# Cross-attention and routed experts on one core: another order of one attention turn on all five engines

## The chip, the cores and the metric

The kernel runs on one core of a Trainium2 chip, as one program on its five engines: TensorE (matmuls and transposes), VectorE, ScalarE, GpSimd and SyncE, which here only issues DMAs. The engines run side by side, each in the order in which its own instructions are written, and wait for each other on semaphores. The metric is the device time of one execution in microseconds, as the median of several.

## What is computed

For x and a context of 64 x 64 rows of 256 numbers:

```python
x = x + attention(layernorm(x), ctx)       # 16 heads of 16, keys and queries RMS-normed
x = x + experts(layernorm(x))              # 8 experts, 2 of them for each row
# attention: q = rms(ln(x) @ Wq + b) * nq;  k = rms(ctx @ Wk + b) * nk;  v = ctx @ Wv + b
#            softmax(q k^T / 4) v, for each head and sequence, then @ Wo + b
# (the text half of the context is empty: 64 rows are fewer than 257)
# experts:   logits = ln(x) @ gate; softmax, best two, weights normed to 1
#            each: (silu(x W1g) * (x W1u)) @ W2, summed with the weights
```

## The kernel before

The 4096 rows are 32 tiles of 128. **Stage one** handles the attention of a tile, picks its experts and sends each row, normed, with its weight, to two places of a buffer in HBM that is sorted by expert. **Stage two** loads that buffer in 72 slots of 128 rows and runs the experts. The change touches stage one alone.

Stage one is a pipeline of 38 **turns**, written out with no planner: `turns_sp` calls each engine's `turn(j, s)`, with turn number i = 4j + s. In one turn an engine works on several tiles, each in another phase. `tile(lag)` is tile i - lag (a negative lag is a tile ahead), on GpSimd and SyncE it is `Tile(j, s - lag)`. The order of the calls in `turn` is the engine's order of work, and nothing else sets it. Buffers are doubled by the tile's parity, so nearly each step also waits until the tile two before it has been read. All matmuls with full precision are done with operands split into a high and a low part: ScalarE makes the high part (`..._hi`), VectorE or GpSimd the low one (`..._lo`).

What a tile passes through, with the names and lines of the profile:

- `ln1_stats`, `ln1_mean` (VectorE, L819, L824) give mean and variance. GpSimd's `ln1` gives the reciprocal root (`inv_sqrt`: an add L413, then a power L415) and the shift (L422). ScalarE's `ln1_norm` (L548) norms.
- `tr_x` (L1134) transposes on TensorE, `xt_hi` (L542) and `xt_lo` (L829) split.
- The context: SyncE's `load_ctx` (L322), ScalarE's `ctx_hi` (L569), GpSimd's `ctx_lo` (L401).
- `project_kv` and `project_q` (L1117 to L1125): queries, keys, values. `k_square`, `q_square` (L593, L599) sum squares on ScalarE. GpSimd's `qk_rms` turns them into **r_qk**, the reciprocal roots for query and key (add L413, 128x2; power L415, 128x2). `k_scale` (ScalarE, L628) and `q_scale` (VectorE, L883) apply it.
- `tr_k` (L1143), `k_hi` (L554), `k_lo` (L835): keys transposed and split. `tr_q` (L1150), `q_hi` (L564, four copies), `q_lo` (L841): the queries. Both use one PSUM bank, so `tr_q` waits until `k_lo` has read the keys.
- `score_max` (L1165): rough scores. `find_max` (L846), `neg_max_hi`, `neg_max_lo` (L852, L857), `tr_max` (L1206), `neg_max_rows` (L586): negated maxima. `score` (L1227 to L1231): the scores with these added. `softmax_exp` (L621).
- SyncE's `spread_v` (L335) lays the values out block by block; `weigh` (L1177) multiplies, `invert_sums`, `normalise` (L864, L870), `tr_att` (L1212), `att_hi`, `att_lo` (L615, L877), `project_out`; `residual` (L892 to L899) adds and takes the second norm's statistics.
- GpSimd's `ln2` (L413, L415), VectorE's `ln2_norm` (L905) and ScalarE's `row_copy` (L581) make the rows. `choose` (L914 to L927, even turns), `count_rows`, `route` (L934 to L949, odd turns) find the places of two tiles. `gap_exp` (L635) and GpSimd's `weights` (L442 to L446) give the expert weights.
- GpSimd's `send` writes the row numbers (L451) and issues two indirect DMAs (L457), one for each of a row's two experts, six turns after the tile's projections.

The expert weights are also loaded and split in stage one, one 32nd a turn (`load_weights`, `weights_hi` L574, `weights_lo` L407).

Of the kernel before, what the change touches and what calls it, by code (L numbers as in the profile page):

```python
# [24 lines left out]
NT = T // P  # L25
# [20 lines left out]
SKEW = 4  # L46
# [39 lines left out]
def build_in(nc, stack, x, ctx_t, w_proj, w_out, w_exp, w_gate, bias, norm_q, norm_k, out,  # L86
# [216 lines left out]
    def _(sp):  # L303
# [39 lines left out]
        def turn(j, s):  # L343
            if Tile(j, s + 2).live:
                load_ctx(Tile(j, s + 2))
# [9 lines left out]

        turns_sp(sp, turn)
# [30 lines left out]
    def _(pool):  # L387
# [22 lines left out]
        def inv_sqrt(t, out_, tmp, in_, scale, eps, ready, mid, done_):  # L410

            need_alone(pool, pool_passed, ready, t.n + 1)
            pool.tensor_scalar(tmp, in_, scale, eps, ALU.mult, ALU.add).then_inc(mid, 1)  # L413
            need_alone(pool, pool_passed, mid, t.n + 1)
            pool.tensor_tensor(out_, tmp, half_neg[:, 0:tmp.shape[1]], ALU.pow).then_inc(done_, 1)  # L415

        def ln1(t):
            need_alone(pool, pool_passed, S["xn_ready"], t.n - 1)
            inv_sqrt(t, rstd[:, t.slot, :], veps[:, t.slot, :], mean_var[:, t.par, 1:2], 1.0, 1e-5,
                     S["ln1_mean"], S["ln1_veps"], S["ln1_rstd"])  # L420
            need_alone(pool, pool_passed, S["ln1_rstd"], t.n + 1)
            pool.tensor_scalar(shift[:, t.par, :], mean_var[:, t.par, 0:1], rstd[:, t.slot, :], -1.0, ALU.mult, ALU.mult  # L422
                               ).then_inc(S["ln1_shift"], 1)

        def qk_rms(t):
# [3 lines left out]
            inv_sqrt(t, r_qk[:, t.par, :], ms_eps[:, t.par, :], sumsq[:, t.par, :], 1.0 / D, 1e-6,  # L429
                     S["k_squared"], S["qk_veps"], S["qk_rstd"])  # L430

        def ln2(t):
            need_alone(pool, pool_passed, S["row_ready"], t.n - 1)
            inv_sqrt(t, rstd2[:, t.slot, :], veps2[:, t.par, :], mean_var2[:, t.par, 1:2], 1.0, 1e-5,
                     S["ln2_mean"], S["ln2_veps"], S["ln2_rstd"])
# [12 lines left out]
        def send(t):  # L448
# [3 lines left out]
                             ).then_inc(S["ids_set"], 1)  # L452
            need_alone(pool, pool_passed, S["ids_set"], t.n + 1)
            need_alone(pool, pool_passed, R["place_set"], t.pair + 1)
            need_alone(pool, pool_passed, R["weight_set3"], t.pair + 1)
            for k in range(2):
                pool.indirect_dma_start(  # L457
                    sorted_rows, bass.IndirectOffsetOnAxis(ap=place_i[:, t.slot // 2, k, t.par:t.par + 1], axis=0),
                    row[:, k, t.slot, :], None, bounds_check=ROWS - 1, oob_is_err=False
                ).then_inc(row_sent[t.slot], 16)  # L460
# [35 lines left out]
        ln1(Tile(0, 0))  # L496
        ln1(Tile(0, 1))
# [21 lines left out]
        for q in (qp_h, qp_l):  # L519
            pool.memset(q[:, :, :, :, :, :].rearrange("p u b c g l -> p (u b c g l)").bitcast(F32), 0.0  # L520
                        ).then_inc(q_cleared, 1)
        turns_sp(pool, turn)
# [15 lines left out]
    def _(act):  # L538
# [99 lines left out]
        def turn(j, s):  # L638
# [7 lines left out]
            if tile(0).live:  # L646
                xt_hi(tile(0))
            if tile(1).live:
                k_hi(tile(1))
            if tile(-1).live:  # L650
                ln1_norm(tile(-1))
            if tile(-1).live:
                ctx_hi(tile(-1))
            if tile(1).live:
                t = tile(1)
                t.first = isinstance(j, int) and t.n == 0
                q_hi(t)
            if tile(2).live:
                neg_max_rows(tile(2))
            if tile(0).live:  # L660
# [3 lines left out]
            if tile(3).live:  # L664
                att_hi(tile(3))
            if tile(0).live:
                v_copy(tile(0))
            if tile(0).live:
                weights_hi(tile(0))
                k_scale(tile(0))  # L670
            if tile(4).live:
                row_copy(tile(4))
            if tile(2).live:
                softmax_exp(tile(2))
            if s % 2 == 1 and tile(5).live:
                gap_exp(tile(5), tile(4), (s - 5) // 2 % 2)
# [16 lines left out]
        ln1_norm(t)  # L693
        split_hi(1)
# [50 lines left out]
    def _(dve):  # L745
# [144 lines left out]
        def residual(t):  # L890
# [5 lines left out]
            dve.bn_stats(stats2[:, t.par, :], x1[:, t.at, :]).then_inc(S["ln2_stats"], 1)  # L896
            need(dve, S["row_ready"], t.n - 1)
# [53 lines left out]
        def turn(j, s):  # L951
# [8 lines left out]
            ahead = tile(-2) if tile(-2).live else None  # L960
            if tile(0).live:
                xt_lo(tile(0))
            if isinstance(j, int) and j == s == 0:
                rest_of_setup()
            if tile(1).live:
                k_lo(tile(1))
            if tile(2).live:
                find_max(tile(2))
            if ahead:
                n = j * SKEW + s + 2 if isinstance(j, int) else None  # L970
                ln1_stats(ahead, {2: x_second, 8: x_third, 9: x_rest}.get(n))
            if tile(2).live:
                neg_max_hi(tile(2))
            if tile(3).live:
                invert_sums(tile(3))
            if tile(2).live:
                neg_max_lo(tile(2))
            if tile(3).live:
                normalise(tile(3))
            if ahead:  # L980
                ln1_mean(ahead)
            if tile(1).live:
                q_lo(tile(1))
            if tile(4).live:
                ln2_norm(tile(4))
# [4 lines left out]
            if isinstance(j, int) and j == s == 0:  # L990
                fold_gate()
            if tile(0).live:
# [453 lines left out]
```

## Time and profile before

| | |
|---|---|
| three runs, median (lowest to highest) | 549.66 us (548.14 to 552.85) |
| the profiled execution | 549.9 us, span 548.1 |
| busy share of the span: TensorE, VectorE, ScalarE, GpSimd | 80%, 75%, 58%, 55% |
| between 250 and 300 us: TensorE, VectorE, ScalarE, GpSimd busy | 45.8, 44.5, 36.7, 36.2 of 50 us, granted clock 1.00 |
| chain that ended last | TensorE 62%, VectorE 12%, issue 7%, ScalarE 5%, GpSimd 5% |
| longest waits, 60 to 310 us | ScalarE q_hi for TensorE tr_q 34.2 us in 27; ScalarE neg_max_rows for tr_max 22.6; GpSimd send for its own row numbers 19.7; GpSimd's r_qk add for the squares 19.5; ScalarE k_scale for r_qk 10.4 |
| one find_max (L846) | 1.22 us |
| one indirect DMA of L457 on GpSimd | 0.97 to 1.25 us, 64 in all |

"Busy" is time in which an instruction of the engine runs. A wait is put down to the engine whose semaphore came last. The first attention turns start near 12 us, the last query transposes are at 313 us, GpSimd's last send ends at 347.8, and stage two ends at 548.

### The profile page before, as it was taken

Reading aid. Unit: us, or ns where it says so; the run is one execution under the profiler, and the core shown is the slowest. Engines: PE = TensorE matmul, PEld = TensorE weight load, DVE = VectorE, ACT = ScalarE, POOL = GpSimd, SP = SyncE. Lnnn points to the kernel's source line nnn. Section 1 sums busy time; section 2 is a strip of 40 time slices with the busy share of each in tenths; the row PEclk is TensorE's granted clock in tenths of the full one; section 3 lists DMA queues with packets and bytes.
Section 4 is the critical chain, followed back from the end, with each engine's and each line's share of the span. In section 5 each row is a group of like instructions: output and inputs, shape, how many; then the busy total and the mean of one; then the engine's idle time right before and its main releaser. Section 6 shows DMA issues by size and latency. Waiting matters only on the chain.

```text
span 548.1 us, 14646 instructions
## 1 busy us (share of the span) xinstructions
PE 438.2 (80%) x4120; PEld 389.1 (71%) x4120; DVE 413.4 (75%) x1359; ACT 315.5 (58%) x934; POOL 303.5 (55%) x531
## 2 busy tenths in 40 slices
PE   2879889898989998898989772299999999999100
PEld 1668778777877877787778661199999999899100
DVE  7458888988988898889888867066767676676384
ACT  5357777767776867686777531155656666565000
POOL 6634467777777677767776646224444444444200
PEclk9989999999999999999999986599999999999655
DMA  7231432222322222222222113524444444331499
GB/s 232 53 111 40 133 129 83 73 65 80 88 67 72 74 82 73 77 78 77 79 72 74 50 50 94 149 81 129 124 123 126 119 121 126 111 115 66 168 401 351
DMA packets 49560, 60.51 MB, mean 110 GB/s; under 512 B 7616, under 2 KB 43083, under 8 KB 49483
## 3 DMA queue, kind: packets, MB, share of 16 engines
q1 hardware_dynamic: 38026, 38.00, 23.7%
q0 software_dynamic: 6528, 16.86, 8.8%
q10 hardware_dynamic: 4928, 4.72, 2.6%
q8 instruction: 37, 0.61, 0.5%
q14 instruction: 41, 0.33, 0.2%
HBM read 32.86 MB, written 23.27 MB: 102 GB/s over the span
## 4 chain that ended last, share of the span: by engine, by line
PE 62%; DVE 12%; issue 7%; ACT 5%; POOL 5%; DMA 4%; SPq 2%; another core or an unknown queue 0%; POOLq 0%; ACTq 0%; DVEq 0%
PE bank L1117 11%; PE bank L1118 11%; PE bank L1119 11%; PE bank L1328 4%; DMA we_l<-expert_out 3%; PE bank L1177 3%; PE bank L1125 3%; PE bank L1150 3%; PE bank L1227 2%; DVE late L835 2%; PE bank L1231 2%; PE bank L1228 2%; PE bank L1229 2%; PE bank L1165 2%; PE bank L1357 1%
## 5 line engine op out<-in xcount | busy, mean ns | idle before, releaser
L527 POOL DMA_INDIRECT expert_out<-probs,late x72 | 70.0, 972 | 94.4 <-ACT probs L720 60.1
L457 POOL DMA_INDIRECT sorted_rows<-row,place_i x64 | 66.0, 1031 | 36.2 <-POOL row L451 24.5
L564 ACT CAST qp_h<-bank 32x256 f16<-32x256 f32 x128 | 46.4, 363 | 40.8 <-PE bank L1150 38.5
L841 DVE TENSOR_TENSOR qp_l<-bank,qp_h 32x256 f16<-32x256 f32 x128 | 53.7, 419 | 9.8 <-ACT qp_h L564 6.6
L1117 PE MATMUL bank<-we_h,xt_h 128*128 x144 | 53.4, 371 | 0.1
L1075 DVE SCALAR_TENSOR_TENSOR probs<-xn,late,bank 128x128 f32<-128x128 f32 x72 | 25.0, 347 | 36.2 <-issue 16.9
L708 ACT ACTIVATE xn<-bank 128x176 f32<-128x176 f32 x72 | 22.9, 318 | 42.7 <-PE bank L1119 35.2
L1118 PE MATMUL bank<-we_l,xt_h 128*128 x144 | 47.1, 327 | 0.0
L1119 PE MATMUL bank<-we_h,xt_l 128*128 x144 | 46.9, 326 | 0.0
L1067 DVE TENSOR_TENSOR xt_l<-bank,xt_h 128x256 fp32r<-128x256 f32 x72 | 30.5, 424 | 21.3 <-ACT xt_h L702 17.5
L1328 PE MATMUL bank<-ident,late 128*128 128x128 f32 x144 | 30.4, 294 | 18.4 <-DMA late<-sorted_rows 16.2
L415 POOL TENSOR_TENSOR rstd<-veps,half_neg 128x1 f32<-128x1 f32 x64 | 36.8, 575 | 5.5 <-POOL veps L413 0.2
L846 DVE TENSOR_REDUCE bank<-bank 128x16 f32<-128x1024 f32 x32 | 39.1, 1221 | 0.0
L702 ACT CAST xt_h<-bank 128x256 fp32r<-128x256 f32 x72 | 27.1, 376 | 18.9 <-PE bank L1328 18.4
L1227 PE MATMUL bank<-qp_h,late 128*128 128x256 f16 x128 | 35.7, 279 | 2.5 <-ACT neg_max_t L586 0.4
L720 ACT COPY probs<-bank 128x256 f32<-128x256 f32 x72 | 26.8, 373 | 17.6 <-PE bank L1358 10.5
L1177 PE MATMUL bank<-v_bd,probs 128*64 128x34 f32 x1024 | 36.0, 225 | 0.2 <-ACT probs L621 0.2
L1231 PE MATMUL bank<-neg_max_t,head_of 128*128 128x128 bf16 x256 | 35.6, 221 | 0.0
L1228 PE MATMUL bank<-qp_l,late 128*128 128x256 f16 x128 | 35.3, 276 | 0.0
L1229 PE MATMUL bank<-qp_h,late 128*128 128x256 f16 x128 | 35.3, 276 | 0.0
L1177 PEld LDWEIGHTS bank<-v_bd,probs 128*64 128x64 f32 x1024 | 32.4, 138 | 3.6 <-ACT probs L621 0.4
L621 ACT ACTIVATE probs<-bank 128x1024 f32<-128x1024 f32 x32 | 32.8, 1025 | 2.3 <-PE bank L1231 2.3
(199 smaller groups left out, 1594.7 us busy)
## 6 DMA issues: line engine op xcount, KB each, us to landing
late<-sorted_rows SPq DMA_DIRECT2D x72, 129.0 KB
we_f<-w_exp SPq DMA_DIRECT2D x32, 152.0 KB
v_bd<-v_sb SPq DMA_DIRECT2D x128, 34.0 KB, 1.9
ctx_in<-ctx_t SPq DMA_DIRECT2D x32, 128.0 KB
we_h<-expert_out SPq DMA_DIRECT2D x8, 512.0 KB, 6.8
we_l<-expert_out SPq DMA_DIRECT2D x8, 512.0 KB, 15.7
x<-x SPq DMA_DIRECT2D x3, 1024.0 KB, 5.8
out<-we_h ACTq DMA_DIRECT2D x8, 256.0 KB, 13.0
```

Source lines behind the costliest of these rows:

```text
L457: pool.indirect_dma_start(sorted_rows, bass.IndirectOffsetOnAxis(ap=place_i[:, t.slot // 2, k, t.par:t.par + 1], axis=0), row[:, k, t.slot ...
L527: pool.indirect_dma_start(expert_out, bass.IndirectOffsetOnAxis(ap=hs[:, r, D:D + 1].bitcast(U32), axis=0), y_sb[:, r % YRING, :], None, b ...
L564: act.copy(q_part(qp_h, t, g), q_bank(g)).then_inc(S["q_h_ready"], 1)
L841: dve.tensor_tensor(q_part(qp_l, t, g), q_bank(g), q_part(qp_h, t, g), ALU.subtract).then_inc(S["q_l_ready"], 1)
L1117: pe.matmul(dst, a_h, b_h, start=start, stop=False)
L1118: pe.matmul(dst, a_h, b_l, start=False, stop=False)
L1119: return pe.matmul(dst, a_l, b_h, start=False, stop=stop)
L1177: ins = pe.matmul(av_bank[b * L:(b + 1) * L, g * 2 * VW:(g + 1) * 2 * VW], probs[:, t.par, at:at + L], v_bd[:, t.par, b, :, g * VW:(g + 1) ...
L1227: pe.matmul(dst, k_h, q_h, start=True, stop=False)
L1228: pe.matmul(dst, k_h, q_l, start=False, stop=False)
L1231: ins = pe.matmul(dst[:, gh * P:(gh + 1) * P], head_of[:, (b * KC + c) * NQ // 2 + gh, :], neg_max_t[:, t.par, :], start=False, stop=gh == ...
L1328: ins = pe.transpose(bank[:, p, c * P:(c + 1) * P], hs[:, r, c * P:(c + 1) * P], ident[:, :])
```

## The change

Each engine's `turn` calls the same steps in another order, and some steps are split so that their halves can stand apart. On GpSimd `inv_sqrt` becomes `add_eps` and `inv_sqrt`; `ln1` becomes `ln1_root` and `ln1_shift`; `ln2` becomes `ln2_veps` and `ln2_root`; `send` becomes `set_ids` and `send(t, k)`, one indirect DMA each. The first send waits for the query transposes of its turn, the second for the scores of the tile before. On VectorE the aggregate of the second norm becomes `ln2_mean`, a turn later. The context is loaded, and split, one turn earlier. Before the turns, `tr_x` and `xt_hi` of tile 0, `ctx_hi` and `ctx_lo` of tile 1 and the load of context 2 are done in advance.

```diff
 # SyncE
-            if Tile(j, s + 2).live:
-                load_ctx(Tile(j, s + 2))
+            if Tile(j, s + 3).live:
+                load_ctx(Tile(j, s + 3))
...
+        load_ctx(Tile(0, 2))
         turns_sp(sp, turn)
 # GpSimd
+        def ln1_root(t):
             need_alone(pool, pool_passed, S["xn_ready"], t.n - 1)
+            add_eps(t, veps[:, t.slot, :], mean_var[:, t.par, 1:2], 1.0, 1e-5, S["ln1_mean"], S["ln1_veps"])
+            inv_sqrt(t, rstd[:, t.slot, :], veps[:, t.slot, :], S["ln1_veps"], S["ln1_rstd"])
...
         def turn(j, s):
-            if Tile(j, s + 1).live:
-                ctx_lo(Tile(j, s + 1))
+            i = j * SKEW + s
+            if Tile(j, s - 6).live:
+                need(pool, S["q_transposed"], min(i, NT))
+                send(Tile(j, s - 6), 0)
+            if Tile(j, s - 4).live:
+                ln2_veps(Tile(j, s - 4))
             if Tile(j, s + 2).live:
-                ln1(Tile(j, s + 2))
+                ctx_lo(Tile(j, s + 2))
+            if Tile(j, s + 2).live:
+                ln1_root(Tile(j, s + 2))
+            if Tile(j, s - 4).live:
+                ln2_root(Tile(j, s - 4))
             if Tile(j, s).live:
                 qk_rms(Tile(j, s))
-            if s % 2 == 0 and Tile(j, s - 6).live:
-                weights(Tile(j, s - 6), Tile(j, s - 5), (s - 6) // 2 % 2)
-            if Tile(j, s - 6).live:
-                send(Tile(j, s - 6))
-            if Tile(j, s - 3).live:
-                ln2(Tile(j, s - 3))
             if Tile(j, s).live:
                 weights_lo(Tile(j, s))
+            if Tile(j, s + 2).live:
+                ln1_shift(Tile(j, s + 2))
+            if Tile(j, s - 6).live:
+                need(pool, S["scored"], min(max(i - 1, 0), NT))
+                send(Tile(j, s - 6), 1)
+            if s % 2 == 1 and Tile(j, s - 5).live:
+                weights(Tile(j, s - 5), Tile(j, s - 4), (s - 5) // 2 % 2)
+            if Tile(j, s - 5).live:
+                set_ids(Tile(j, s - 5))
```

The other three, as the order of the calls in one turn (the number is the lag):

```
ScalarE  before: xt_hi 0, k_hi 1, ln1_norm -1, ctx_hi -1, q_hi 1, neg_max_rows 2, k_square 0, q_square 0,
                 att_hi 3, v_copy 0, weights_hi 0, k_scale 0, row_copy 4, softmax_exp 2, gap_exp (odd)
         after:  q_hi 1, weights_hi 0, neg_max_rows 2, ctx_hi -2, k_square 0, q_square 0, att_hi 3,
                 ln1_norm -1, v_copy 0, gap_exp (odd), k_scale 0, softmax_exp 2, row_copy 4, k_hi 0, xt_hi -1
VectorE  before: xt_lo 0, k_lo 1, find_max 2, ln1_stats -2, neg_max_hi 2, invert_sums 3, neg_max_lo 2,
                 normalise 3, ln1_mean -2, q_lo 1, ln2_norm 4, att_lo 3, route (odd), gate_of_x 0,
                 q_scale 0, residual 3, choose (even)
         after:  k_lo 1, xt_lo 0, find_max 2, ln2_mean 4, neg_max_hi 2, neg_max_lo 2, invert_sums 3,
                 ln1_mean -2, ln1_stats -3, normalise 3, q_lo 1, att_lo 3, route (odd), ln2_norm 4,
                 q_scale 0, gate_of_x 0, residual 3, choose (even)
TensorE  before: tr_x 0, tr_k 1, score_max 2, weigh 3, tr_q 1, project_kv 0, project_q 0, tr_max 2,
                 count_rows (odd), tr_att 3, score 2, project_out 3
         after:  weigh 3, score_max 2, tr_q 1, project_kv 0, tr_max 2, project_q 0, count_rows (odd),
                 tr_att 3, score 2, project_out 3, tr_k 0, tr_x -1
```

## Rows read from the trace of the kernel before

**Rows 1.** TensorE in time order, turn 7 (start, length in us; [idle before]).
```profile
80.77 0.41 PE L1150 MATMUL bank<-ident,late 128*128 128x128 f32 x2 [0.91 <-issue]
```

**Rows 2.** TensorE in time order, turns 25 to 27.
```profile
248.60 0.41 PE L1150 MATMUL bank<-ident,late 128*128 128x128 f32 x2 [0.92 <-DVE late L835]
...
257.71 0.41 PE L1150 MATMUL bank<-ident,late 128*128 128x128 f32 x2 [0.17 <-issue]
...
259.60 0.28 PE L1117 MATMUL bank<-wp_h,xt_h 128*128 128x264 f32 x1
...
264.81 0.61 PE L1165 MATMUL bank<-late,qp_h 128*128 128x128 f16 x8 [0.29 <-ACT probs L621]
...
265.35 1.13 PE L1177 MATMUL bank<-v_bd,probs 128*64 128x34 f32 x32
...
267.39 0.41 PE L1150 MATMUL bank<-ident,late 128*128 128x128 f32 x2 [0.92 <-DVE late L835]
```

**Rows 3.** ScalarE in time order, turns 25 and 26.
```profile
249.38 1.52 ACT L564 CAST qp_h<-bank 32x256 f16<-32x256 f32 x4 [1.97 <-PE bank L1150]
...
258.16 1.52 ACT L564 CAST qp_h<-bank 32x256 f16<-32x256 f32 x4 [0.53 <-PE bank L1150]
...
260.71 0.27 ACT L586 COPY neg_max_t<-bank 128x128 bf16<-128x128 bf16 x1 [1.03 <-PE bank L1206]
...
262.11 0.48 ACT L574 CAST we_h<-we_f 128x304 fp32r<-128x304 f32 x1
...
262.98 0.47 ACT L628 ACTIVATE late<-bank,r_qk 128x256 f32<-128x256 f32 x1 [0.38 <-POOL r_qk L415]
...
263.64 1.03 ACT L621 ACTIVATE probs<-bank 128x1024 f32<-128x1024 f32 x1
...
265.79 0.42 ACT L569 CAST ct_h<-ctx_in 128x256 fp32r<-128x256 f32 x1
```

**Rows 4.** GpSimd in time order, turns 24 to 26.
```profile
247.72 0.98 POOL L457 DMA_INDIRECT sorted_rows<-row,place_i  x1 [0.30 <-issue]
...
252.85 0.36 POOL L413 TENSOR_SCALAR ms_eps<-sumsq 128x2 f32<-128x2 f32 x1 [0.43 <-ACT square L599]
...
259.04 0.73 POOL L401 TENSOR_TENSOR ct_l<-ctx_in,ct_h 128x256 fp32r<-128x256 f32 x1
...
261.95 0.19 POOL L413 TENSOR_SCALAR ms_eps<-sumsq 128x2 f32<-128x2 f32 x1 [0.80 <-ACT square L599]
...
262.23 0.71 POOL L415 TENSOR_TENSOR r_qk<-ms_eps,half_neg 128x2 f32<-128x2 f32 x1
...
262.92 0.19 POOL L442 TENSOR_SCALAR one_e<-e_gap 128x2 f32<-128x2 f32 x1
...
265.11 1.10 POOL L457 DMA_INDIRECT sorted_rows<-row,place_i  x1 [0.81 <-POOL row L451]
...
267.83 0.58 POOL L415 TENSOR_TENSOR rstd<-veps,half_neg 128x1 f32<-128x1 f32 x1
...
268.39 0.83 POOL L407 TENSOR_TENSOR we_l<-we_f,we_h 128x304 fp32r<-128x304 f32 x1
```

**Rows 5.** VectorE in time order, end of turn 26.
```profile
263.90 0.42 DVE L892 TENSOR_TENSOR x<-bank,x 128x256 f32<-128x256 f32 x1 [0.45 <-PE bank L1125]
...
264.89 0.18 DVE L899 BATCH_NORM_AGGREGATE mean_var<-stats 128x2 f32<-128x6 f32 x1
...
266.23 0.42 DVE L829 TENSOR_TENSOR xt_l<-bank,xt_h 128x256 fp32r<-128x256 f32 x1
...
266.57 0.68 DVE L835 TENSOR_TENSOR late<-bank,late 128x512 f16<-128x512 f32 x1
```

**Rows 6.** VectorE in time order, ln2_norm in turn 25.
```profile
252.75 0.41 DVE L905 TENSOR_SCALAR row<-x,mean_var,rstd 128x256 f32<-128x256 f32 x1
```

**Rows 7.** The end of the stage: VectorE's last aggregate, GpSimd's last send.
```profile
334.20 0.18 DVE L899 BATCH_NORM_AGGREGATE mean_var<-stats 128x2 f32<-128x6 f32 x1
...
346.84 0.97 POOL L457 DMA_INDIRECT sorted_rows<-row,place_i  x1 [0.30 <-issue]
```

More of the change, by code:

```diff
@@ L495, in _ @@
                                  base=0, pattern=[[1, NE], [-1, NE]], channel_multiplier=0))
-        ln1(Tile(0, 0))
-        ln1(Tile(0, 1))
+        for n in range(2):
+            ln1_root(Tile(0, n))
+            ln1_shift(Tile(0, n))
         ctx_lo(Tile(0, 0))
@@ L521, in _ @@
                         ).then_inc(q_cleared, 1)
+        ctx_lo(Tile(0, 1))
         turns_sp(pool, turn)
@@ L657, in turn @@
                 q_hi(t)
+            if tile(0).live:
+                weights_hi(tile(0))
             if tile(2).live:
                 neg_max_rows(tile(2))
+            if tile(-2).live:
+                ctx_hi(tile(-2))
             if tile(0).live:
@@ L665, in turn @@
                 att_hi(tile(3))
+            if tile(-1).live:
+                ln1_norm(tile(-1))
             if tile(0).live:
                 v_copy(tile(0))
+            if s % 2 == 1 and tile(5).live:
+                gap_exp(tile(5), tile(4), (s - 5) // 2 % 2)
             if tile(0).live:
-                weights_hi(tile(0))
                 k_scale(tile(0))
+            if tile(2).live:
+                softmax_exp(tile(2))
             if tile(4).live:
                 row_copy(tile(4))
[L673 to L676, printed above, removed]
+            if tile(0).live:
+                k_hi(tile(0))
+            if tile(-1).live:
+                xt_hi(tile(-1))
         def split_hi(n):
@@ L693, in _ @@
         ln1_norm(t)
+        xt_hi(t)
+        ctx_hi(Tile(0, 1))
         split_hi(1)
@@ L989, in turn @@
                 route(tile(5), tile(4), (s - 5) // 2 % 2)
-            if isinstance(j, int) and j == s == 0:
+            if tile(4).live:
+                ln2_norm(tile(4))
+            if n == 0:
                 fold_gate()
             if tile(0).live:
+                q_scale(tile(0))
+            if tile(0).live:
                 gate_of_x(tile(0))
-                q_scale(tile(0))
             if tile(3).live:
@@ L1293, in turn @@
                 score_max(t)
-            if tile(3).live:
-                weigh(tile(3))
             if tile(1).live:
                 tr_q(tile(1))
-            if tile(0).live:
+            if static and i == 0:
                 t = tile(0)
-                t.first = static and i == 0
-                for project_next in (project_q, project_kv) if t.first else (project_kv, project_q):
-                    project_next(t)
-            if static and i == 0:
+                t.first = True
+                project_q(t)
+                project_kv(t)
                 gate_fold()
+            elif tile(0).live:
+                t = tile(0)
+                t.first = False
+                project_kv(t)
             if tile(2).live:
@@ L1308, in turn @@
                 tr_max(t)
+            if tile(0).live and not (static and i == 0):
+                t = tile(0)
+                t.first = False
+                project_q(t)
             if s % 2 == 1 and tile(5).live:
@@ L1318, in turn @@
                 project_out(t)
+            if tile(0).live:
+                tr_k(tile(0))
+            if tile(-1).live:
+                tr_x(tile(-1))
         gate_mean()
+        tr_x(Tile(0, 0))
         turns_sp(pe, turn)
```

76 lines of the change are left out of this document (33 added, 43 removed).

## The prediction

> **What bounds the kernel now.** I read the table of slices first: from about 45 to 313 us the attention turns run, one tile a turn, with TensorE and VectorE both near nine tenths busy and the granted clock at full speed. No engine is full there, so the question is which chain of waits sets one turn. I call T the start of the query transposes in a turn. From turn 7 to turn 27 TensorE starts them every (267.39 - 80.77) / 20 = 9.33 us [rows 1, 2], 18.66 a pair: 9.11 from turn 25 to 26 and 9.68 from 26 to 27 [rows 2]. The chain of waits and the list of waits then show the loop inside one turn [rows 2 to 5]. ScalarE takes the queries at T + 0.45 and the squares after the maxima; GpSimd gives r_qk at T + 5.23 (262.94); both ScalarE (k_scale) and VectorE (q_scale) stand waiting for it. ScalarE then does k_scale, row_copy and the exponential (starts 0.66 after k_scale, takes 1.03). TensorE is released 0.14 later, does 0.54 of score_max and the weighing, and could go on. It waits for VectorE's k_lo, which ends 0.14 before T [rows 5]. So both the exponential and k_lo hang on r_qk, and GpSimd's order of work is what to watch. One pair of sends costs GpSimd 0.81 + 1.10 + 0.30 + 0.98 = 3.2 us a turn; in the present order it stands behind r_qk [rows 4], where it holds up nobody in the loop.
>
> **Rearrangement on TensorE, ScalarE and VectorE.** No instruction is added on these three; each turn keeps its matmuls and copies. What leaves the loop: row_copy moves behind the exponential (0.29: of the 0.66 from k_scale's start to the exponential's, k_scale takes its 0.47 less 0.10); xt_lo (0.34, 266.23 to 266.57) moves behind k_lo; the second aggregate (0.18 with 0.10 in front of it) moves from the residual into the next turn. The weighing now comes before score_max, but the query transposes stand behind both in either order, so that swap is worth nothing to T. What enters: find_max now starts only after score_max. It starts at about T + 0.1 and takes 1.22 (table of the profile), its two negations some 0.4 more (estimate), done by T + 1.75, and TensorE needs them after transposes and key/value projection, at T + 1.89 (259.60 - 257.71). So that costs nothing, but with 0.1 of cover.
>
> **The new chain to r_qk.** ScalarE: queries at T + 0.45, 1.52 long, so 1.97. Then weights_hi (0.48), neg_max_rows (0.27), each less the 0.10 by which neighbours overlap, and ctx_hi (0.42): 2.93. The old order did ctx_hi at the end of the turn, in idle time [rows 3]. GpSimd may start ctx_lo at 2.97. Its order is now ctx_lo (0.73 + 0.09), the first norm's add (0.28) and power (0.58), the second norm's power (0.58), and only then the add (0.28, 261.95 to 262.23) and power (0.71) of r_qk [rows 4]: 2.97 + 0.82 + 0.28 + 0.58 + 0.58 + 0.28 + 0.71 = **T + 6.22**, where it was T + 5.23. The squares are ready near T + 3.7, since nothing in front of them grew, so they do not end last.
>
> If the context half did not end last, the first send would: it waits for the query transposes (T + 0.45), then needs 0.81 and 1.10, the second norm's add 0.28, and the same chain of 3.25: T + 5.89. That is the lower bound. GpSimd's whole turn is queued behind this new wait, and ScalarE, VectorE and TensorE wait for that turn's r_qk.
>
> SyncE's context load moves one turn ahead and the first of them in front of the turns. The copy that reads it comes a turn minus some 5 us later, so a load that lands late has more room than before; its issue slot (0.6 us of SyncE) delays nothing that is awaited. Both at nothing.
>
> **From r_qk to the next T.** Exponential path: 0.04 + 0.37 (k_scale) + 1.03 + 0.14 + 1.06 of weighing (1.13, less the 0.07 by which score_max's 0.61 overlaps it) + 0.54 = 3.18 [rows 2, 3], so T' = 9.40, against 9.11 now. VectorE path in the even turn, where the experts are chosen: 0.04 + q_scale 0.38 (as k_scale) + gate_of_x 0.18 (an estimate by the aggregate, the nearest small row) + (266.57 - 263.90 = 2.67, less 0.28 and 0.34) 2.05 + k_lo 0.68 + 0.14 = 3.47, so T' = 9.69, against 9.68 [rows 5]. In the odd turn this path is shorter by the choosing (266.23 - 264.89 - 0.10 = 1.24) and does not end last. A bare pair is 19.09.
>
> **GpSimd after r_qk.** weights_lo 0.80 (268.39, 0.83 long) and the shift reach T + 7.0. The wait for the scores asks for something finished near T + 5, so it costs nothing. The second send starts 0.3 to 0.81 after the last small instruction is handed over; I take 0.81 from the shift's start, 7.8, and it ends at 8.9. In odd turns the weights (262.92 to 265.11 - 1.00, so 1.19) bring 10.1, and set_ids with the first send's start (0.19 + 0.81) 11.1 = T' + 1.7. That send ends at T' + 2.8, the small add at 3.07, against 2.97 for the context half: 0.10 late (0 to 0.5), in the even turn. Splitting the sends thus saves none of their price: 0.30 becomes up to 0.81.
>
> **A collision.** ln2_norm on VectorE is released by the second norm's power, which now is the instruction just before the add of r_qk. In the present trace these meet once in each odd turn: while ln2_norm (0.41) runs, the add takes 0.36 instead of 0.19 [rows 4, 6]. I take that 0.17 for the even turn; in the odd turn routing puts VectorE's half later, behind slack. The bounds are 0 and 0.35.
> The Trainium skill ("SBUF — State Buffer", section "Who interferes with whom") says that a VectorE tensor_scalar from SBUF to SBUF can take the port pair it shares with GpSimd, and that the later of the two fully blocks. By that rule, the trace agrees: 252.85 + 0.36 is 0.05 after ln2_norm's end. Taken at its word, the two would start within 0.05 of each other in every even turn, the loser would wait a whole instruction, and the sum below would be 2 us higher than with 0.17.
>
> **The sum.** Even turn 9.69 + 0.10 + 0.17 = 9.96; pair 19.36, 0.70 above 18.66. Sends are there from turn 6, contexts end with turn 29: 12 pairs, **+8.4**. Start: the first r_qk gets ctx_hi (0.42) and part of ctx_lo (0.73) in front of it, +1.0 with the first five turns taken as even (0 to +3). End: turns 30 and 31 have no context and no first norm, so r_qk falls back to the squares and each gains some 0.55, -1.1. After the last aggregate GpSimd now needs 13.4 us to the end of the last send (334.38 to 347.81) [rows 7]; then 0.9 for the root, 0.5 + 0.97 for the send left over, 1.19 weights, and for the last two tiles 2 x (1.00 + 1.05 + 0.30 + 0.97) = 6.6: 10.2 to 10.5. But the aggregate itself stands behind the choosing (1.24), and find_max comes 0.5 earlier without k_lo's queue: -2.0 (-4 to 0). Total: 549.9 (the profiled execution, span 548.1 and 1.8 around it) + 1.0 + 8.4 - 3.1 = **556.2**. The median of the runs is 0.2 below the profiled time, so I say 556. The second stage is untouched and only starts later or earlier.
>
> **Rivals.**
> *Faster.* If r_qk stayed at T + 5.23 (the context copy and the two roots are hidden, or a release is sooner than I have it), the same edits pay: odd turn 5.23 + 3.18 = 8.41; even turn, VectorE's residual waits for TensorE as now (T + 6.19) and gives 6.19 + 2.05 + 0.82 = 9.06; pair 17.47, -1.19, and 549.9 + 1.0 - 14.3 - 3.1 = 533.5. TensorE's 0.9 us of idle before the odd T [rows 2] speaks for it; the order written in the diff speaks against. It makes the kernel faster by over 1% once r_qk comes before T + 5.87 with no lateness or collision. Chance 0.12.
> *No change.* At the lower bound T + 5.89, without extras, the pair is 18.43: -2.8 over the stage, -2.1 outside it, 545; up to 552 at r_qk's 6.22 less one of the two extras and with the end's better bound. Chance 0.25.
> *Slower still.* In turn 25 ScalarE began the queries 0.78 after T, not 0.45 as in turn 26: 0.68 after the end of the second send (247.72 + 0.98) [rows 2 to 4]. If a send holds back what ScalarE waits for until 0.68 after its end, the first send (T + 1.26 to 2.36, or to 2.8) now holds neg_max_rows until T + 3.0 or 3.5 instead of 2.35: +0.7 and +1.1 a pair, less the 0.1: 19.36 + 1.7 = 21.1, 549.9 + 12 x 2.4 - 2.1 = 577. For it: ScalarE stood idle for 1.97 there, so nothing of its own kept it. Against: in turn 26, also behind two sends, it began at the usual 0.45. Chance 0.13, with all from 565 up.
> *It does not do what it says.* The wait for the scores never holds anything back (T + 5 against 7.0), so the second send stands where GpSimd's own queue puts it. The time is that of the forecast.
>
> **How the numbers follow.** Forecast case, 552 to 565: chance 0.50. About 1% (5.5 us) is what a measurement tells from no change. Faster: the first rival, 0.12. Slower: the third, 0.13, and of the forecast case what lies above 555.2, 0.35, so 0.48. The rest, 0.40, is within 1%. The range leaves out the first rival and the upper part of the third: 545 (the no-change rival's lower end) to 567 (lateness 0.5, collision 0.35: pair 19.94, +15.4; start +3, end 0 beside the -1.1).
>
> **What would show it.** After the change: r_qk's end at T + 6.2 in both turns; ctx_lo starting at once behind ctx_hi; ScalarE and VectorE idle about 2 us for r_qk; TensorE idle over 1 us before the weighing and none, or 0.3 in odd turns, before the query transposes; pairs of 19.1 to 19.5; the last send some 2 us nearer to the last aggregate. Wrong if r_qk comes before T + 5.8, or if the squares, not the queue before r_qk, end last.

## The result, and the profile after

The changed kernel takes 559.3 us (median of 4 runs, 556.8 to 562.4), the kernel before 549.1 (4 runs on the same chip). The ratio is 1.018, with a 95% interval of 1.014 to 1.022: slower by 1.8%. The profiled execution took 559.5, with a span of 557.8 (before 548.1). Forecast were 556 and a range of 545 to 567.

TensorE in time order, turns 7 and 25 to 27 (start, length in us; [idle before]); these answer [rows 1, 2]:

```profile
82.20 0.41 PE L1180 MATMUL bank<-ident,late 128*128 128x128 f32 x2 [0.42 <-DVE late L861]
...
256.50 0.41 PE L1180 MATMUL bank<-ident,late 128*128 128x128 f32 x2 [0.36 <-DVE late L861]
...
265.97 0.41 PE L1180 MATMUL bank<-ident,late 128*128 128x128 f32 x2
...
275.86 0.41 PE L1180 MATMUL bank<-ident,late 128*128 128x128 f32 x2 [0.35 <-DVE late L861]
```

These are the starts T of the query transposes. From turn 7 to 27 a pair of turns takes (275.86 - 82.20) / 10 = 19.37 us, where it took 18.66: odd to even 9.47, even to odd 9.89. TensorE no longer stands 0.92 before the odd T; its idle time has moved to the key transposes, behind k_scale. GpSimd in turn 25, which answers [rows 4]:

```profile
257.71 0.98 POOL L467 DMA_INDIRECT sorted_rows<-row,place_i  x1 [2.21 <-PE bank L1180]
258.76 0.19 POOL L414 TENSOR_SCALAR veps<-mean_var 128x1 f32<-128x1 f32 x1
259.61 0.73 POOL L402 TENSOR_TENSOR ct_l<-ctx_in,ct_h 128x256 fp32r<-128x256 f32 x1 [0.66 <-ACT ct_h L592]
260.43 0.19 POOL L414 TENSOR_SCALAR veps<-mean_var 128x1 f32<-128x1 f32 x1
260.70 1.09 POOL L419 TENSOR_TENSOR rstd<-veps,half_neg 128x1 f32<-128x1 f32 x2
261.88 0.19 POOL L414 TENSOR_SCALAR ms_eps<-sumsq 128x2 f32<-128x2 f32 x1
262.15 0.75 POOL L419 TENSOR_TENSOR r_qk<-ms_eps,half_neg 128x2 f32<-128x2 f32 x1
...
264.10 1.06 POOL L467 DMA_INDIRECT sorted_rows<-row,place_i  x1 [0.17 <-issue]
```

Read it downwards: the first send waits 2.21 for TensorE, but what ends last is the context copy, 0.66 later; from there GpSimd has no gap until r_qk, which ends at 262.90, T + 6.40 (before: T + 5.23). ScalarE in the same turn, which answers [rows 3]:

```profile
256.94 1.52 ACT L587 CAST qp_h<-bank 32x256 f16<-32x256 f32 x4 [1.48 <-PE bank L1180]
258.49 0.45 ACT L597 CAST we_h<-we_f 128x304 fp32r<-128x304 f32 x1
258.96 0.27 ACT L609 COPY neg_max_t<-bank 128x128 bf16<-128x128 bf16 x1
259.12 0.41 ACT L592 CAST ct_h<-ctx_in 128x256 fp32r<-128x256 f32 x1
...
262.93 0.47 ACT L651 ACTIVATE late<-bank,r_qk 128x256 f32<-128x256 f32 x1 [0.56 <-POOL r_qk L419]
263.30 1.02 ACT L644 ACTIVATE probs<-bank 128x1024 f32<-128x1024 f32 x1
```

The copy (ct_h) stands behind three others. In the list of waits of turns 7 to 27, k_scale's wait for r_qk is 21.9 us over 20 turns, q_scale's 12.3, and TensorE's for k_scale 17.5. In the chain that ended last GpSimd, 5% before, now has 16%:

```profile
PE 39%; issue 18%; POOL 16%; DVE 12%; DMA 5%; ACT 5%; SPq 3%; POOLq 0%; ACTq 0%; DVEq 0%
```

The span is 9.7 longer: 1.1 until turn 6 (72.23 against 71.09), 8.6 from turn 6 to 30 (232.43 against 223.87), and nothing behind turn 30, where 3.1 less were forecast.

### The profile page after: what moved, and what is told of

Same layout as the page of the kernel before. It is cut to its first block, busy times and chain, and to the rows that moved or that the text cites. A ratio compares the mean times of both kernels' runs of the same rounds, so it can differ in the third digit from the quotient of the medians.

```text
span 557.8 us, 14742 instructions
## 1 busy us (share of the span) xinstructions
PE 442.1 (79%) x4120; PEld 389.6 (70%) x4120; DVE 407.8 (73%) x1359; ACT 321.0 (58%) x934; POOL 304.1 (55%) x531
## 4 chain that ended last, share of the span: by engine, by line
PE 39%; issue 18%; POOL 16%; DVE 12%; DMA 5%; ACT 5%; SPq 3%; POOLq 0%; ACTq 0%; DVEq 0%
PE bank L1147 8%; PE bank L1148 7%; PE bank L1149 7%; POOL ct_l L402 4%; POOL r_qk L419 4%; PE bank L1366 4%; DMA we_l<-expert_out 3%; POOL rstd L419 3%; DVE late L861 2%; POOL veps L414 2%; ACT probs L644 2%; PE bank L1385 2%; POOL sorted_rows L467 2%; PE bank L1180 1%; PE bank L1396 1%
## 5 line engine op out<-in xcount | busy, mean ns | idle before, releaser
L467 POOL DMA_INDIRECT sorted_rows<-row,place_i x64 | 67.3, 1051 | 59.9 <-PE bank L1180 30.8
L1366 PE MATMUL bank<-ident,late 128*128 128x128 f32 x144 | 30.4, 294 | 18.9 <-DMA late<-sorted_rows 17.1
L1173 PE MATMUL bank<-ident,late 128*128 128x128 f32 x128 | 21.1, 288 | 28.8 <-ACT late L651 28.8
L402 POOL TENSOR_TENSOR ct_l<-ctx_in,ct_h 128x256 fp32r<-128x256 f32 x32 | 23.4, 732 | 31.8 <-ACT ct_h L592 30.8
L1173 PEld LDWEIGHTS bank<-ident,late 128*128 128x128 f32 x128 | 13.6, 141 | 34.9 <-ACT late L651 34.9
L419 POOL TENSOR_TENSOR rstd<-veps,half_neg 128x1 f32<-128x1 f32 x64 | 35.4, 560 | 3.2
L1257 PE MATMUL bank<-qp_h,late 128*128 128x256 f16 x128 | 35.8, 280 | 0.0
```

Source lines behind the costliest of these rows:

```text
L402: pool.tensor_tensor(ct_l[:, t.par, :, :], src, ct_h[:, t.par, :, :].bitcast(F32), ALU.subtract).then_inc(S["ct_ready"], 1)
L419: pool.tensor_tensor(out_, in_, half_neg[:, 0:in_.shape[1]], ALU.pow).then_inc(done_, 1)
L467: pool.indirect_dma_start(sorted_rows, bass.IndirectOffsetOnAxis(ap=place_i[:, t.slot // 2, k, t.par:t.par + 1], axis=0), row[:, k, t.slot ...
L1366: ins = pe.transpose(bank[:, p, c * P:(c + 1) * P], hs[:, r, c * P:(c + 1) * P], ident[:, :])
```

## The experiments

All times are medians of 4 to 10 runs against the kernel before on the same chip (548.9 to 550.3 in these sessions), in three batches. T is as above, r_qk the end of its power, both from the profiled execution, turns 7 to 27. "Pair" is the time of two turns. The granted clock over these turns is 1.00 in all kernels but e5 (0.98) and e6 (0.87), so the columns of these two mix waits with a slower TensorE.

| kernel | us | ratio (95%) | pair | r_qk - T, odd / even |
|---|---|---|---|---|
| before | 549.1 | 1 | 18.66 | 5.26 / 5.25 |
| changed | 559.3 | 1.018 (1.014 to 1.022) | 19.37 | 6.40 / 6.38 |
| e1 | 541.1 | 0.984 (0.977 to 0.991) | 18.19 | 5.01 / 6.17 |
| e2 | 545.4 | 0.992 (0.989 to 0.995) | 18.61 | 5.88 / 6.15 |
| e3 | 578.1 | 1.050 (1.043 to 1.058) | 20.45 | 6.69 / 7.13 |
| e4 | 559.2 | 1.018 (1.011 to 1.025) | 19.37 | 6.40 / 6.39 |
| e5 | 590.0 | 1.072 (1.067 to 1.078) | 21.53 | 7.15 / 6.71 |
| e6 | 608.4 | 1.105 (1.099 to 1.111) | 23.57 | 7.32 / 8.02 |
| e7 | 535.9 | 0.974 (0.971 to 0.978) | 17.82 | 5.06 / 5.78 |
| e8 | 540.7 | 0.981 (0.975 to 0.987) | 18.18 | 5.05 / 6.41 |
| e9 | 531.3 | 0.967 (0.964 to 0.971) | 17.46 | 5.02 / 5.19 |
| e10 | 533.9 | 0.973 (0.970 to 0.976) | 17.75 | 5.02 / 5.73 |
| e11 | 559.3 | 1.019 (1.015 to 1.022) | 19.48 | 6.40 / 6.41 |
| e12 | 564.7 | 1.029 (1.025 to 1.032) | 19.58 | 6.40 / 6.37 |

**e1, r_qk ahead of the context.** GpSimd's turn in the changed kernel:

```diff
 ln2_veps(s - 4)
-ctx_lo(s + 2)
-ln1_root(s + 2)
 ln2_root(s - 4)
 qk_rms(s)
+ctx_lo(s + 2)
+ln1_root(s + 2)
 weights_lo(s)
```

> The changed kernel with one thing moved: on GpSimd the second norm's power and then the add and power of r_qk come right behind the second norm's add, and the subtraction of the context (ctx_lo) and the first norm's add and power follow behind them. Theory (GpSimd's queue in front of r_qk sets the turn): the squares end near T + 3.9, so r_qk ends at T + 4.9 instead of 6.4; then ScalarE's own work up to k_scale (it stood idle 1.04 a turn for r_qk) ends last, near T + 5.4, and VectorE's 0.6 a turn is used up: odd turn 8.5, even turn 9.3, pair 17.7 to 18.1, 541 us (537 to 547). Rival (GpSimd is nearly full, what it does behind r_qk only comes back as lateness in the next turn): the pair stays at 18.9 to 19.4, 553 to 560. Rival (order of TensorE and VectorE sets the turn): r_qk comes sooner but the waits move to TensorE, 556 to 560.

541.1: the theory's time. GpSimd's queue in front of r_qk is what made the change slow; with three instructions (ctx_lo and the first norm's add and power) behind r_qk instead of before it, the same change is faster than the kernel before. The pair (18.19) is longer than forecast, all of it in the even turn, so the time is met in part by luck: 4.2 of the 20.0 us that the span lost against the changed kernel lie before turn 6 (T of turn 6 at 68.02, not 72.23), which the forecast doesn't name. GpSimd in the even turn:

```profile
248.70 1.07 POOL L467 DMA_INDIRECT sorted_rows<-row,place_i  x1 [0.16 <-issue]
249.81 0.21 POOL L450 TENSOR_SCALAR one_e<-e_gap 128x2 f32<-128x2 f32 x1
...
251.05 0.19 POOL L459 COPY row<-result_row 128x2 int32<-128x2 int32 x1
252.10 1.08 POOL L467 DMA_INDIRECT sorted_rows<-row,place_i  x1 [0.86 <-POOL row L459]
253.26 0.19 POOL L414 TENSOR_SCALAR veps<-mean_var 128x1 f32<-128x1 f32 x1
253.53 0.57 POOL L419 TENSOR_TENSOR rstd<-veps,half_neg 128x1 f32<-128x1 f32 x1
254.18 0.19 POOL L414 TENSOR_SCALAR ms_eps<-sumsq 128x2 f32<-128x2 f32 x1
```

T is 249.01. There is no wait left in this stretch: the queue comes late out of the odd turn, and 0.86 goes by before a send whose ids have just been set. That is the second rival, in one half of the pair. ScalarE's late queries (T + 1.22 in this turn) aren't the reason: in turn 20 they start at T + 0.42, and r_qk still ends at T + 6.22.

**e2, the context copy early.** ScalarE's ctx_hi goes to the end of its turn, ctx_lo takes the tile s + 1 that is then ready, and the ctx_lo of tile 1 ahead of the turns goes:

```diff
 neg_max_rows(2)
-ctx_hi(-2)
 ...
 xt_hi(-1)
+ctx_hi(-2)
# GpSimd
-ctx_lo(s + 2)
+ctx_lo(s + 1)
```

> The changed kernel with ScalarE's context copy (ctx_hi) moved back to the end of its turn, as it stood in the kernel before, so that GpSimd's ctx_lo finds it done. Theory (the context copy in front is the release that ends last): the first send ends near T + 2.3, and the same chain behind it gives r_qk at T + 5.7 to 5.9; pair 18.1 to 18.6, 544 to 550 us. This is the lower bound of the prediction. Rival (the copy's place is hidden by the send's wait and by the squares): r_qk stays within 0.15 of T + 6.4, 556 to 561.

545.4, as the theory had it: the odd turn's r_qk at T + 5.88 is the prediction's lower bound (5.89) almost to the digit. The even turn's came 0.27 later, GpSimd being late there.

**e3, the sends joined.**

```diff
-need(q_transposed); send(s - 6, 0)
 ...
 ln1_shift(s + 2)
+need(scored); send(s - 6, 0)
 send(s - 6, 1)
```

> The changed kernel with a tile's two sends together again, both where the second stands (behind the first norm's shift and the wait for the scores). All else as changed. Theory (the split is worth nothing; ctx_lo waits for the context copy and not for the send): r_qk stays at T + 6.3 to 6.4, pair 19.3 to 19.5, 557 to 561 us. Rival (the split is what keeps GpSimd from being late): GpSimd's work behind r_qk grows by 1.3, in the odd turn into the next one, and the time is 564 or more. Rival (the first send in front costs the loop something, by its wait or by what it holds up): 552 or less.

578.1: the time lies in the first rival's range, but the reasons that I expected were all wrong. GpSimd wasn't late (ctx_lo still waits 1.05 for the copy). What moved was ScalarE, and VectorE with it. The second send, T of turn 26, the copy of the queries and find_max, from the timelines of GpSimd, TensorE, ScalarE and VectorE:

```profile
276.62 0.97 POOL L467 DMA_INDIRECT sorted_rows<-row,place_i  x1 [0.30 <-issue]
```
```profile
277.10 0.41 PE L1178 MATMUL bank<-ident,late 128*128 128x128 f32 x2
```
```profile
278.33 0.75 ACT L585 CAST qp_h<-bank 32x256 f16<-32x256 f32 x2 [1.82 <-PE bank L1178]
```
```profile
278.29 1.23 DVE L870 TENSOR_REDUCE bank<-bank 128x16 f32<-128x1024 f32 x1 [1.00 <-PE bank L1193]
```

The copy of the queries waits for the transposes alone and starts 0.45 after T elsewhere. Here it starts at T + 1.23, in odd turns at T + 0.77, each time 0.72 to 0.76 after the end of the second send. The two delays, 0.33 and 0.78, are 1.11, and the pair grew by 1.08. VectorE's find_max, which waits for score_max, is late too: T + 1.18 here and T + 0.72 in odd turns, where the changed kernel has T + 0.12 and T + 0.10. In the kernel before ScalarE's queries show the same in the odd turns (T + 0.78, 0.68 after the second send).

**e4, no order waits.**

```diff
-need(q_transposed)
 send(s - 6, 0)
 ...
-need(scored)
 send(s - 6, 1)
```

> The changed kernel without the two waits that only order: neither send waits for TensorE (not for the query transposes, not for the scores). The sends then go out as soon as GpSimd's queue reaches them. Theory: r_qk stays at T + 6.3 to 6.4 since ctx_lo still waits for the context copy; 557 to 561 us, and GpSimd's 28 us of waits for the query transposes turn into a longer wait for the context copy. Rival (a send that starts before T holds back k_lo or q_hi, which the wait was there to prevent): T slips by 0.3 to 0.7 a turn, 565 to 575.

559.2, pair 19.37: the two waits cost and bring nothing in the changed kernel. The first send of the odd turn was in flight over T there (T - 0.19 to T + 0.79) and the queries started at T + 0.45 all the same. So not every send in flight holds ScalarE.

**e5, the old kernel with the copy in the loop.**

```diff
# ScalarE, kernel before
-ctx_hi(-1)
 q_hi(1)
 neg_max_rows(2)
+ctx_hi(-1)
```

> The kernel before with one thing moved: ScalarE's context copy (ctx_hi) from the end of its turn to behind the negated maxima, where the change puts it. GpSimd's order stays (ctx_lo, the first norm's add, power and shift, then r_qk). Theory (this one move is what makes the change slow): ctx_lo can't start before T + 2.97, and with 0.82 + 0.28 + 0.58 + 0.28 + 0.28 + 0.71 behind it r_qk ends at T + 5.9 to 6.0 instead of 5.25; pair 19.7 to 20.1, 560 to 566 us. Rival (the squares end last, the copy is hidden): r_qk stays at T + 5.3, 548 to 552.

590.0: the direction of the theory, its size far off. I had taken the time of the copy from the changed kernel's order. In the old one it starts at T + 3.15, ctx_lo at T + 3.64, and r_qk ends at T + 6.7 to 6.9. Turn 23, ScalarE:

```profile
262.51 0.27 ACT L586 COPY neg_max_t<-bank 128x128 bf16<-128x128 bf16 x1 [0.24 <-PE bank L1206]
262.67 0.41 ACT L569 CAST ct_h<-ctx_in 128x256 fp32r<-128x256 f32 x1
```

In three of the odd turns (13, 19, 25) it is worse, because the granted clock falls: in turn 25 it is 0.50 until 2.4 us after T, neg_max_rows waits 1.40 for TensorE, the copy starts at 285.03, T + 4.29, and r_qk ends at 288.66, T + 7.9. These turns are 1.1 longer than the other odd ones, some 3 us in all. One move of an instruction of 0.41 costs 40 us, and the clock explains little of it.

**e6, only the sends apart in the old kernel.** GpSimd's turn rewritten, the other engines as before:

```diff
+need(q_transposed); send(s - 6, 0)
 ctx_lo(s + 1); ln1(s + 2); qk_rms(s)
-weights; ids; send(s - 6, both)
 ln2(s - 3)
 weights_lo(s)
+need(scored); send(s - 6, 1)
+weights(s - 5, s - 4); set_ids(s - 5)
```

> The kernel before with only GpSimd's queue changed: the first send at the start of the turn behind the query transposes, the second behind its weights_lo and the scores, weights and ids behind it. ScalarE, VectorE and TensorE keep their old order. Theory: the old odd turns lose 0.33 because ScalarE's queries start 0.78 after T behind two joined sends (0.45 elsewhere); with the sends apart they start at T + 0.45 in both turns, and the first send ends at T + 2.2 to 2.4, so that r_qk ends by T + 5.3; pair 18.2 to 18.6, 543 to 549 us. Rival (a send in front of r_qk costs what it takes, whatever the other engines do): r_qk at T + 5.6 or later, 553 or more.

608.4: a poor experiment that still says something. The sends used to fill the time until VectorE's second mean; without them GpSimd's ln2 stood 2.04 a turn for it (40.8 us over turns 7 to 27), with weights_lo, the second send, the ids and the next turn's ctx_lo behind it. And TensorE got a lower clock with it (this kernel and the one before, turns 7 to 27: us, TensorE's busy time, granted clock, DMA share, GB/s):

```profile
81.77:317.44 235.67, 195.36 (x1891) 0.87 0.21 60
```
```profile
80.77:267.39 186.62, 169.09 (x1890) 1.00 0.26 76
```

The one pair at full clock, from turn 20 to turn 22, takes 21.65 (mean of all: 23.57), and in its odd turn r_qk ends at T + 5.42, close to the theory's 5.3; in the other odd turns the add of r_qk waits up to 2.0 for the squares. So about 3.0 of the 4.9 by which the pair grew are waits and the rest goes with the clock, an estimate from one pair. Splitting the sends in this queue alone is ruinous. That the change could do it because it also moved VectorE's mean and took ln2 a turn later fits, but no run tests it. The price of the split itself can't be read from this run.

**e7, the second norm's roots ahead of the first send** (from e1):

```diff
-need(q_transposed); send(s - 6, 0)
 ln2_veps(s - 4)
 ln2_root(s - 4)
+need(q_transposed); send(s - 6, 0)
 qk_rms(s)
```

> The faster version (r_qk ahead of the context) with the first send moved behind the second norm's add and power. Theory (a send whose condition is already true starts 0.16 after the instruction before it, one with a fresh condition 0.8 to 0.9; GpSimd is full in the odd-to-even half, where r_qk came at T + 6.17): 0.6 to 0.8 less before r_qk in the even turn, so T + 5.4 to 5.6 there, if the send in flight at T still makes ScalarE start the queries at T + 1.2; pair 17.4 to 17.8, 531 to 536 us. Rival (the start of a send costs 0.8 wherever it stands): pair stays at 18.1 to 18.3, 539 to 542.

535.9, and a pair of 17.82: the theory's ranges, at their upper ends, since r_qk came at T + 5.78 in the even turn and not at 5.4 to 5.6. A send with a condition that has just come true starts after 0.86 to 0.96 of idle time in e1, one whose conditions are older after 0.15 to 0.64 in e7. The order put the wait beside other work.

**e8, the second send behind r_qk** (from e7), and **e9, the same without the waits**:

```diff
 qk_rms(s)
+need(scored); send(s - 6, 1)      # e9: no need()
 ctx_lo(s + 2)
 ...
 ln1_shift(s + 2)
-need(scored); send(s - 6, 1)
```

> As the run before it, and the second send moved from behind the first norm's shift to right behind r_qk, so that no send is in flight while TensorE does the query transposes. Theory (a send in flight at T holds back ScalarE's queries): they start at T + 0.45 in both turns, r_qk ends at T + 5.3 to 5.5 in the even turn; pair 17.1 to 17.5, 528 to 533 us, 2 to 5 less than without this move. Rival (the late start of the queries has another cause, or is slack): no difference from the run without it, within 2 us.

> The version with the second send right behind r_qk, now without the two waits that only order. There GpSimd stood 1.04 for the scores in the odd turn, with its whole queue behind it, and r_qk came at T + 6.41 in the even turn. Theory (GpSimd's queue in the odd-to-even half is what is left, so the wait passes through in full): r_qk at T + 5.4 in the even turn, pair 17.1 to 17.4, and some 2 to 3 us less in the last turns, where the waits keep the second norm's roots back: 525 to 531 us. Rival (VectorE or TensorE ends last by now): pair stays at 17.8 or more, 535 to 540.

e8 missed: the queries did start at T + 0.45 in every turn (in e7 at T + 1.2 in some even turns), but it was 4.8 slower. The wait for the scores, free at the old place, now held the queue in the odd turn:

```profile
247.11 0.72 POOL L419 TENSOR_TENSOR r_qk<-ms_eps,half_neg 128x2 f32<-128x2 f32 x1
248.87 1.07 POOL L467 DMA_INDIRECT sorted_rows<-row,place_i  x1 [1.04 <-PE bank L1261]
```

Without it, e9:

```profile
237.44 0.72 POOL L419 TENSOR_TENSOR r_qk<-ms_eps,half_neg 128x2 f32<-128x2 f32 x1
238.36 1.07 POOL L467 DMA_INDIRECT sorted_rows<-row,place_i  x1 [0.19 <-issue]
```

The even turn's r_qk went from T + 6.41 to 5.19, and the time from 540.7 to 531.3, the best of all: 3.3% below the kernel before (0.964 to 0.971). The pair of 17.46 is just over the range I gave, since VectorE now ends last in both turns. The chain that ended last in e9:

```profile
PE 52%; DVE 23%; issue 10%; DMA 6%; POOL 3%; SPq 3%; ACT 3%; POOLq 0%; DVEq 0%; ACTq 0%
```

**e10, e7 without the waits.**

> The version with the second norm's add and power ahead of the first send and the second send behind the shift, now without the two waits. Both were over before GpSimd came to them in the running turns. Theory: pair 17.8 as before, and only the last turns get shorter, by 2 to 3 us: 532 to 535 us. Rival (the waits are free everywhere): 535 to 537. Rival (a send in flight at T costs more once nothing orders it): 538 or more.

533.9 (532.8 to 535.2) against e7's 535.9 (533.9 to 537.2), which ran in another batch: 2 us, with ranges that overlap, and the ratios to the kernel before in each batch are 0.973 and 0.974. The pair is the same to 0.07. A difference between the two isn't shown, so this run doesn't decide between its first two forecasts; it rules out the third.

**e11, TensorE's order, and e12, row_copy**, each alone from the changed kernel:

```diff
# e11, TensorE          # e12, ScalarE
-weigh(3)               +row_copy(4)
 score_max(2)            softmax_exp(2)
+weigh(3)               -row_copy(4)
```

> The changed kernel with TensorE's first two steps swapped back: score_max before the weighing, as in the kernel before. Theory (the query transposes stand behind both in either order): r_qk at T + 6.4 and pair 19.3 to 19.5, 557 to 561 us, with find_max starting 1.1 earlier and TensorE waiting for the exponential between the two. Rival (the new order lets TensorE hide score_max, or loses it): 3 us or more to one side.

> The changed kernel with ScalarE's row_copy back in front of the exponential. Theory: the exponential starts 0.29 later. In the odd turn its path ends last (T' = r_qk + 3.07), so that half grows by 0.29; in the even turn VectorE's path (r_qk + 3.5) has 0.3 to 0.4 to spare over it, so nothing: pair 19.6 to 19.7, 561 to 564 us. Rival (both halves hang on the exponential): pair 19.95, 565 to 568. Rival (VectorE's path sets both): no difference, 557 to 561.

e11: 559.3, the swap is worth nothing in time. e12: 564.7; odd half 9.70 (+0.23), even half 9.88 (no change), so the odd turn does end on the exponential's path and the even turn does not. The time is 0.7 above my range; its last turns took 25.8 where the changed kernel's took 23.5 (below).

## Why the prediction was right, and where it was not

**The chain to r_qk** was right, 0.17 short: T + 6.22 forecast, 6.39 measured. In turn 25 ScalarE's context copy ends at 259.53, T + 3.03 (I had 2.93), ctx_lo starts at T + 3.11 (2.97), and from there to r_qk's end it is 3.29 (3.25). That the context copy ends last, and not the send, is shown by both e2 (take it away, the send's bound appears) and e4 (take the send's wait away, nothing happens).

**From r_qk to T** was right in both halves: forecast 3.18 and 3.47, measured 9.47 - 6.40 = 3.07 and 9.89 - 6.38 = 3.51. e12 shows which path is which.

**Lateness and collision** were wrong, both nothing where I had 0.10 and 0.17. The second send started 0.17 after the shift, not 0.55, and the next first send at T + 1.52 instead of 1.70. For the collision, in turn 25:

```profile
261.88 0.19 POOL L414 TENSOR_SCALAR ms_eps<-sumsq 128x2 f32<-128x2 f32 x1
```
```profile
261.93 0.41 DVE L933 TENSOR_SCALAR row<-x,mean_var,rstd 128x256 f32<-128x256 f32 x1
```

They start 0.05 apart, as in every turn from 7 to 27, and both take their usual time. The reading behind the term was wrong as well. In the kernel before the two overlap in all eleven odd turns from 7 to 27, and the add takes 0.36 in turn 25 alone, the one that I had read; in the other ten it takes its 0.19, as in turn 23:

```profile
234.24 0.19 POOL L413 TENSOR_SCALAR ms_eps<-sumsq 128x2 f32<-128x2 f32 x1 [0.42 <-ACT square L599]
```
```profile
234.16 0.42 DVE L905 TENSOR_SCALAR row<-x,mean_var,rstd 128x256 f32<-128x256 f32 x1
```

The Trainium skill ("SBUF — State Buffer", section "Who interferes with whom") says that a tensor_scalar can enter a mode that takes both of VectorE's port pairs, that the later of the two engines blocks when VectorE is in it, and that a tensor_tensor has no such mode. Here ln2_norm takes 0.41 and the residual's tensor_tensor of the same size 0.42 [rows 5, 6], so no row shows ln2_norm in that mode. The trace shows no block, so it neither agrees with the rule nor tests it, and what made the one add 0.36 long stays open.

So the pair, 19.36 forecast and 19.37 measured, is partly two errors that cancel: 0.17 a turn too short, 0.27 too long in the even one.

**The end** is the term that was mis-sized: -3.1 forecast, 0 measured. Turns 30 and 31 did gain (T of turn 30 to T of turn 32: 17.02 against 18.49, -1.5) and so did the sends behind the last aggregate (11.2 against 13.4, -2.2). Against them stand 2.6 more between T of turn 32 and the last aggregate, and 1.4 more between the last send and stage two's first load (3.7 against 2.3).

The 1.4 is a path that the prediction left out. Before the first load SyncE reads the start rows of twelve slots into its registers (`row_of`), one after the other; the profile names what it reads `square`. Before and changed (length in ns: shortest/median/longest; first and last start), each with the first load:

```profile
L361 SPq TENSOR_LOAD <-square x12: 261/268/546, 342.5 to 349.3; - x12
350.13 0.91 SPq L364 DMA_DIRECT2D late<-sorted_rows  x2
```
```profile
L362 SPq TENSOR_LOAD <-square x12: 262/273/529, 352.5 to 359.3; - x12
360.18 0.91 SPq L365 DMA_DIRECT2D late<-sorted_rows  x2
```

The reads take 7.1 us in both kernels, and the load follows the last of them by 0.5. In the kernel before the last send's data lands at 349.4, just before the last read ends (349.6); in the changed one it lands at 358.0 and the reads end at 359.6. So from the last aggregate to the first load it is 14.96 against 15.75: of the 2.2 that the sends gained, stage two got 0.8.

TensorE over the stretch from T of turn 32 to the last aggregate, windows of the kernels before, changed, e4 and e12 (us, TensorE's busy time, granted clock, DMA share, GB/s):

```profile
313.45:334.38 20.93, 13.29 (x151) 0.91 0.12 40
```
```profile
321.68:345.22 23.54, 15.26 (x152) 0.75 0.12 41
```
```profile
321.44:342.12 20.68, 11.73 (x152) 0.95 0.14 47
```
```profile
326.11:351.90 25.79, 17.50 (x152) 0.66 0.11 37
```

The same 151 or 152 matrix operations, and among the kernels with the changed order the stretch is longer the lower the granted clock: also 21.6 at 0.91 (e8), 22.4 at 0.83 (e2), 24.7 at 0.71 (e9), with e3 (27.8 at 0.67) off that line. The old order is shorter at a like clock: 20.9 against e8's 21.6 at 0.91, 22.0 (e5) against 23.6 (e7) at 0.77 and 0.76. So 0.7 to 1.5 of the 2.6 go with the order and the rest with the clock, an estimate from these pairs of kernels. Here TensorE works in bursts between idle time, and the clock falls to its lower level (0.50, 1.2 GHz) for parts of it. Two windows of 3 us of the changed kernel, one mostly idle and the next fully busy at the lower level:

```profile
330.70:333.70 3.00, 1.10 (x14) 1.00 0.12 44
333.70:336.70 3.00, 3.00 (x20) 0.50 0.02 5
```

I had sized this stretch as if the clock stayed as it was. What decides the clock in one execution stays open: e4 and e9 both lack the waits and have 0.95 and 0.71, so it isn't the waits alone. With one profile for each kernel, whether the change brings the lower clock isn't shown either.

**The rivals.** *No change*: its lower bound is a real kernel (e2), but not this one. *Faster*: not this kernel, because of the written order, as argued; the edits do pay once r_qk comes early (e1: 541; e9: 531 against the 533.5 that I gave for it). *Slower still*: the mechanism exists, the case did not occur. A pair of sends close together keeps ScalarE's queries until 0.6 to 0.8 after its end: 0.33 a pair of turns in the kernel before, 1.11 in e3. In the changed kernel every send ends at least 0.8 before T or starts more than 1.2 after it, and the queries start at T + 0.44 in every turn. So the split does bring something, against what the prediction said: with the sends joined the new order is at 578 (e3). That this is near the 577 that I gave for this rival is luck, since I had it from a late neg_max_rows and a pair of 21.1, and e3 has late queries and 20.45. *It does not do what it says*: the wait for the scores never binds in the running turns; e4 shows it.

## What to carry to other kernels

Write down, for each engine's queue, what stands between the last release and the value that the other engines wait for. Here one copy of 0.41 us and three GpSimd instructions behind it, in front of one add and power, turned a gain of 1.6% (e1) into a loss of 1.8%. A wait that only orders is free where the queue arrives late, or where what stands behind it would wait longer anyway (the first send waits 2.21 in the changed kernel, and taking that away in e4 gains nothing). Where neither holds it moves the whole queue behind it (1.04 a pair of turns in e8, r_qk at T + 6.41 instead of 5.19). And a bound that the prediction works out for "if this were not there" is a candidate to run: e2 and e1 were read off it.

## What the runs showed of the hardware

- An indirect send on GpSimd starts 0.81 to 0.87 after the row numbers that it needs (1.06 in one turn of e4), 0.15 to 0.40 after an instruction that it doesn't wait for (up to 0.67 behind the second norm's power in e7 and e8), 0.30 behind another send. Its own length is 0.97 to 1.12 in the running turns.
- Two sends 0.30 apart keep ScalarE's next copy, which waits for TensorE alone, until 0.57 to 0.77 after the second one's end (kernel before, e3, e5), and in e3 VectorE's find_max as well. A single send in flight over T sometimes does the same (e1, e7: T + 1.2 in some even turns, T + 0.42 in others) and sometimes not (e4, all odd turns; e10, all even turns). A single send that ends at T + 0.12 holds nothing in e1's odd turns (queries at T + 0.45), where the second of a pair that ends at T + 0.01 does in e3 (T + 0.77). In e3, e5 and the kernel before SyncE's load of v_bd started within 0.1 of the copy in most of these turns. What is held, and by what, was not found.
- The time from the last send to stage two's first load is 2.0 to 2.3 in the kernel before, e3, e5 and e7 to e10, and 3.7 in the changed kernel, e1, e2, e4, e11 and e12. It isn't the sends' own latency: the last data lands 1.5 to 2.0 after the last send, and the load follows SyncE's twelve register reads (6.8 to 7.1 us together) by 0.5. These begin 5.3 to 5.4 before the end of the last send in the first group and 3.6 to 3.9 before it in the second. Only in e6, where they begin 6.7 before it, does the load wait for the data (1.7).
- TensorE's granted clock fell to its lower level (0.50, 1.2 GHz) in turns 7 to 27 of e5 and e6 alone, the two slowest kernels. In e6 TensorE waits 2.2 for k_scale in ten of the turns; at the lower level a 128x512 matmul takes 0.63 there, where it takes 0.40 at full clock.
